# Two self-attentions of a decoder: the second half of each round of heads placed one quarter later

## What is computed

```
q, k, v = split_heads(x @ Wqkv + b)
att = softmax(q @ k.T / sqrt(8))          # per batch entry and head, 256 x 256
y   = att @ v
x   = x + merge_heads(y) @ Wproj + b
```

## The kernel before, in words

| quarter | TensorE | ScalarE | VectorE |
|---|---|---|---|
| 0 | S, T, W of group it-3 | exponential, copy of F | maxima |
| 1 | S, T, every fourth round R | exponential, copy of W | maxima |
| 2 | S, T, M of group it-1, B of group it-3 | exponential | maxima, shift |
| 3 | S, T, F of group it+2 | exponential | maxima, division |

## Time and profile before

### The profile page before, as it was taken

One profiled execution on the slowest core, in us unless ns is written; L12 is line 12 of the kernel. 1 busy time (PEld: TensorE's weight loads), 2 busy tenths in 40 slices (PEclk: granted clock), 3 DMA queues, 4 the chain that ended last, 5 costly groups with the idle time before them and its releaser, 6 DMA issues.

```text
span 939.7 us, 19518 instructions
## 1 busy us (share of the span) xinstructions
PE 847.7 (90%) x6498; PEld 695.7 (74%) x6498; DVE 561.1 (60%) x1561; ACT 480.4 (51%) x1154; POOL 256.1 (27%) x541
## 2 busy tenths in 40 slices
PE   5999879999999999999999968885897888887788
PEld 3888668888888888888888756663796566665565
DVE  3876466555655566655655347774544577666474
ACT  2455465555555555555555315664464476677141
POOL 3864120000000000000000047551075577776110
PEclk9999999999999999999999989999899899999995
DMA  7000000000000000000000030001222000000000
GB/s 270 2 2 1 1 1 1 1 1 1 0 0 0 0 0 0 0 0 0 0 0 0 1 115 1 2 1 28 88 47 59 1 1 0 0 0 0 24 1 22
DMA packets 9410, 15.85 MB, mean 17 GB/s; under 512 B 816, under 2 KB 5040, under 8 KB 8976
## 3 DMA queue, kind: packets, MB, share of 16 engines
q1 hardware_dynamic: 8400, 13.23, 4.2%
q0 software_dynamic: 960, 1.97, 0.9%
HBM read 13.16 MB, written 2.03 MB: 16 GB/s over the span
## 4 chain that ended last, share of the span: by engine, by line
PE 76%; ACT 7%; DVE 6%; issue 6%; POOL 3%; DMA 1%; ACTq 1%; DVEq 0%; POOLq 0%; SPq 0%
PE psum L875 9%; PE psum L887 9%; PE psum L855 5%; PE psum L856 5%; PE psum L857 5%; PE psum L847 5%; PE psum L598 4%; ACT arena L1301 4%; PE psum L840 3%; PE psum L617 3%; PE psum L635 3%; PE psum L956 2%; PE psum L566 1%; PE psum L1034 1%; PE psum L648 1%
## 5 line engine op out<-in xcount | busy, mean ns | idle before, releaser
L1818 DVE TENSOR_REDUCE xnegmax<-psum 128x1 f32<-128x768 f32 x128 | 122.4, 956 | 139.5 <-PE psum L857 139.3
L1405 ACT ACTIVATE arena<-psum,xnegmax 128x768 f32<-128x768 f32 x128 | 115.5, 903 | 139.5 <-DVE xnegmax L1818 97.8
L2265 POOL COPY acur<-A_all 128x128 f32 (+1 forms) x18 | 5.2, 293 | 388.1 <-PE psum L840 388.1
L875 PE MATMUL psum<-pack_a,arena 128*128 128x128 f32 x768 | 106.8, 275 | 0.2 <-ACT arena L1396 0.2
L1249 ACT ACTIVATE arena<-psum 128x384 f32<-128x384 f32 (+1 forms) x128 | 69.5, 546 | 71.2 <-PE psum L620 42.1
L855 PE MATMUL psum<-kv_high,xq_high 128*128 128x384 f32 x256 | 101.5, 396 | 1.8 <-DVE kv_low L1813 1.6
L875 PEld LDWEIGHTS psum<-pack_a,arena 128*128 128x128 f32 x768 | 87.5, 141 | 13.9 <-issue 12.3
L1396 ACT ACTIVATE arena<-psum 128x512 f32<-128x512 f32 x128 | 75.9, 593 | 42.5 <-PE psum L875 42.5
L887 PE MATMUL psum<-arena,xv 128*64 128x256 f32 x768 | 89.9, 383 | 0.0
L856 PE MATMUL psum<-kv_low,xq_high 128*128 128x384 f32 x256 | 86.8, 339 | 0.0
L857 PE MATMUL psum<-kv_high,xq_low 128*128 128x384 f32 x256 | 86.7, 339 | 0.0
(11 more groups left out here) (309 smaller groups left out, 1853.6 us busy)
## 6 DMA issues: line engine op xcount, KB each, us to landing
w1all<-in_w SPq DMA_DIRECT2D x1, 2048.0 KB, 8.2
arena<-in_w SPq DMA_DIRECT2D x1, 2048.0 KB, 10.8
pack_v<-in_pack_v SPq DMA_DIRECT2D x1, 1088.0 KB, 9.0
pack_l<-in_pack_l SPq DMA_DIRECT2D x1, 1079.5 KB, 12.0
pack_q<-in_pack_q SPq DMA_DIRECT2D x1, 1024.0 KB, 6.9
pack_a<-in_pack_a SPq DMA_DIRECT2D x1, 653.0 KB, 6.1
pack_f<-in_pack_f SPq DMA_DIRECT2D x1, 556.0 KB, 9.9
x<-in_x SPq DMA_DIRECT2D x2, 256.0 KB, 3.0
```

What stands on the lines that cost most here:

```text
L875: last = transpose(bank[4 + (3 * u + c) % 2][:, (2 * i + h) * P:(2 * i + h + 1) * P], xprob[:, u % 2, h * KEYS + kt * P:h * KEYS + (kt + 1 ...
L1405: activation(xprob[:, u % 2, half * KEYS:(half + 1) * KEYS].rearrange("p (c w) -> p c w", c=2), src, ACT.Exp, bias=xnegmax[:, u % 2, half: ...
L1818: v.tensor_reduce(xnegmax[:, u % 2, half:half + 1], banks_pair(half), AX.XY, ALU.max, negate=True)\
```

## The change

TensorE's `LAG` goes from 8 to 9 heads. W moves from quarter 0 to quarter 1, R from 1 to 2, M and B from 2 to 3. On ScalarE the exponentials follow `LAG`, and the copies of W and R move from quarter 1 to 2. On VectorE the shift moves from quarter 2 to 3, right behind M's new place, and the division from quarter 3 of a round to quarter 1 of the next. VectorE's loop gets one more round for it. S, F, the copy of F and all of GpSimd's work stay in place, and no DMA moves.

```diff
-LAG = 8
+LAG = 9
...
-                        if j == 0 and 0 <= it - 3 < H:
+                        if j == 1 and 0 <= it - 3 < H:
                             weighted(it - 3)
-                        if j == 1 and it >= 7 and (it - 7) % G == 0:
+                        if j == 2 and it >= 7 and (it - 7) % G == 0:
                             result_turned((it - 7) // G)
...
-                        if j == 2 and 0 <= it - 1 < H:
+                        if j == 3 and 0 <= it - 1 < H:
                             maxima_turned(it - 1)
-                        if j == 2 and 0 <= it - 3 < H:
+                        if j == 3 and 0 <= it - 3 < H:
...
                             back_to_tokens(it - 3)
...
-                        if j == 1 and 0 <= it - 3 < H:
+                        if j == 2 and 0 <= it - 3 < H:
                             empty_weighted(it - 3)
-                        if j == 1 and it >= 7 and (it - 7) % G == 0:
+                        if j == 2 and it >= 7 and (it - 7) % G == 0:
                             result_ready((it - 7) // G)
...
-                for it in range(H + 3):
+                for it in range(H + 4):
...
-                        if j == 2 and 0 <= it - 1 < H:
+                        if j == 3 and 0 <= it - 1 < H:
                             shifted_queries(it - 1)
-                        if j == 3 and 0 <= it - 3 < H:
-                            divided(it - 3)
+                        if j == 1 and 0 <= it - 4 < H:
+                            divided(it - 4)
```

## The result

The changed kernel takes **947.06 us**, the median of 10 runs (945.04 to 954.7), against 941.12 for ten runs of the kernel before beside it. Of both kernels some runs last about 8 us longer than the rest (of the ten, three after the change and one before), and without those the medians are 946.04 and 941.05, +5.0 us; two runs of the kernel before beside later experiments, of 1631 and 1669 us, are left out throughout.

The account below looks back on a forecast made before the run. The prediction took TensorE's queue to bound the kernel, with waits for ScalarE in attention 1. It added 3.5 us for W's wait and 0.3 for the ends to 941.05, giving 944.9 us, range 942.7 to 947.0.

Parts of the forecast that it names:

- W's wait, twelve rounds, 3.5 us: Attention 1, rounds 3 to 14: with F moved, W waits for ScalarE's exponential, +0.29 us a round, 3.5 us.
- M's wait stays: Attention 1: M still starts 1.39 us after the first T behind W, behind ScalarE's copy; gain none.
- Faster: Rival, 0.06: in attention 1 the quarter's delay, not the copy, releases M's hole; -5.0 us, 936.1 us.
- Hidden: Rival, 0.10: W waits at no cost in attention 1, queue or exponential being quicker; only the ends remain, 941.3 us.
- The ends of attention 1, +0.12: Attention 1's first and last rounds: early S costs no time, missing S gives 0.24 back, P before T adds 0.36.
- Attention 0, +0.21: Attention 0's end: P in round 16 now precedes T, +0.21 us; its main rounds cost 0.
- slower still: Rival, 0.06: attention 0's 0.22 us to spare is eaten, W waits about 0.2 us in 12 rounds, 947.3 us.
- the division's move: VectorE: the division gets two quarters instead of one, with the next B a whole round away; no cost.
- 3.5 + 0.3 = +3.8 us: Whole kernel: attention 1's twelve rounds plus the ends of both attentions, added to the median 941.05, give 944.9 us.
- cut a little: Range: 943.3 to 946.5, widened by half the three runs' 1.84 us spread either side, trimmed to 942.7 to 947.0.

Follow-up runs that it names:

- The repeat: The changed kernel timed once more, unaltered, against the kernel before: 946.84 us, ratio 1.0031, beside 941.7 us.

## Why the prediction was right in its steps and short in its size

The direction, the cause and nearly every term held, and 947.06 still lies just outside the range that ended at 947.0.

- *W's wait, twelve rounds, 3.5 us.* Measured: +0.29 for the first (9.61 to 9.90) and +3.13 for the eleven others, 3.42. T to W is 1.09 us, as taken from the earlier trace rows, and F's own place is the cause.
- *M's wait stays.* Right: 1.40 us behind T, 11 holes, 5.5 us. Right also that the copy behind the exponential sets it, which removing that order proved. "Faster" falls: M's hole wasn't the split's. The Trainium skill, "Perfetto Trace Analysis", in Matmuls, asks for independent groups to rotate through different PSUM banks, so that the emptying of one overlaps the products of the next. The trace agrees: M and W share bank 5, and M stands idle for 5.5 us behind W's copy. Here turning two instructions around on ScalarE was enough; another bank wasn't tried.
- *"Hidden".* Refuted: the drained end's row was the geometry of every round.
- *The ends of attention 1, +0.12.* Measured +0.28. W of round 15 to 16 went from 4.62 to 4.38 us (the missing S, -0.24, as forecast); the next went from 4.42 to 4.94, +0.52 instead of +0.36: P starts 0.22 us behind B, where T started 0.13 behind it, and T to W is 1.17 us instead of 1.09 (B, P, T and W start at 645.25, 645.47, 646.28 and 647.45).
- *Attention 0, +0.21.* Measured +0.35, the end +0.22 of it. The rounds were costed at 0 and grew by 0.13; W doesn't wait there, so "slower still" didn't come about by W. What the prediction costed at nothing was the division's move ("covered by the same distance"), and it named B as the one that would wait. It was R of round 7. VectorE's timeline after, with the statistics of the context that now precede the division:

```profile
56.59 0.38 DVE L1545 BATCH_NORM_AGGREGATE stat<-moments 128x2 f32<-128x6 f32 x4
...
57.92 0.20 DVE L1629 RECIPROCAL arena<-psum 128x8 f32<-128x8 f32 x1
58.16 0.23 DVE L1633 TENSOR_TENSOR arena<-psum,arena 128x64 f32<-128x64 f32 x1
```

and the wait of TensorE's weight load for R, from 57 to 59 us:

```profile
PEld psum L666 <- DVE arena L1633: 0.3, 1, 0.3
```

The two loops together: 0.35 + 0.29 + 3.13 + 0.28 = 4.05 us against 3.8 in the sum. The mean span of three traces of the kernel before is 939.3 us, that of four of the changed one 944.8: +5.5, of which the loops are 4.1 and the operand stretch 1.3 (mean 7.67 before, 8.97 after); 0.1 is left.

**The step that failed** is the sum's last: "3.5 + 0.3 = +3.8 us", set straight on the median, takes everything behind the loops as unchanged. The stretch behind attention 0 can run at either clock level and took 1.58 us more or so at the lower (8.72 against 7.14); no term and no bound stood for it, and in the traces it makes 1.3 of the 5.5 us. Whether the change brings that or the executions fell so stays open. The second miss is in the range: half the spread of three runs (1.84 us) was taken as what a measurement adds, and even that was "cut a little", from 947.4 to 947.0; the ten of the changed kernel spread over 9.7 us, and with that their median can move by 1 us. The repeat's 946.84 would have lain inside the range, so on which side of its end the median fell is luck. That 5.0 to 5.9 us were measured where 3.8 were forecast is the miss.

## What to carry to other kernels

In an in-order queue, independent work between a producer and the instruction that waits for another engine's answer is cover: before moving a step, count what stands between the two and compare that with the latency, here 1.09 us from T to W, of which an S and a T cover 0.88 and F the rest. When a wait shows, look first at what the answering engine does in between: putting one copy ahead of one exponential shortened the span from 939.7 to 926.8 us, by three times what the change lost in the two loops. And a busy share says little: TensorE counted as busy for 60.04 of 60.34 us in attention 0's rounds, yet the copy's place took 2.4 us out of them.

## What the chip showed that was not expected

**One level or the other for the same work.** After attention 0, TensorE is about half busy for 4 us, at a granted clock of 1.00, in both kernels. Windows of the kernel before and of the changed one:

```profile
112.00:116.00 4.00, 2.14 (x25) 1.02 (x23) 2.71 (x13) 1.05 (x3) 1.27 (x2) 1.00 0.02 4
117.30:119.33 2.03, 2.03 (x34) 1.86 (x33) 1.81 (x9) 0.79 (x2) 0.00 (x0) 1.00 0.01 4
```

```profile
112.00:116.00 4.00, 2.10 (x25) 0.99 (x23) 0.86 (x4) 1.09 (x3) 0.00 (x0) 1.00 0.02 4
117.36:120.88 3.52, 3.52 (x33) 3.35 (x32) 2.94 (x13) 1.08 (x2) 1.17 (x2) 0.55 0.01 2
```

The same 2.1 us of work ahead, and the products behind run at 1.00 (2.4 GHz) in one and mostly at the lower level (1.2 GHz) in the other. The Trainium skill, "TensorE: Matmul & The Clock Gate", Part 1, calls the number of slow products at a kernel's start run-variable, puts their cost at under 1% of a typical kernel's span, and advises against fitting to a count. Here the stretch lies inside the kernel; the size agrees (1.5 of 940 us is 0.16%), but in this pair of traces it was a quarter of the change's effect (1.58 of 5.7 us of span).

**Two stretches near the end.** TensorE's level also varies in the last stage, from layer 1's self-attention to the end. In the profiled execution of the changed kernel with the copy first it took 216.8 us, against 208.5 in the kernel before; the changed kernel with F ahead of W and the copy first shows 216.8 too. Windows over the self-attention part, of the kernel before and of the changed one with the copy first:

```profile
731.25:886.49 155.24, 128.36 (x1056) 98.78 (x1056) 102.16 (x450) 93.42 (x309) 98.53 (x228) 0.98 0.01 4
722.57:881.62 159.05, 132.29 (x1057) 102.57 (x1057) 102.14 (x450) 93.40 (x309) 98.54 (x228) 0.96 0.01 4
```

and over the last 28 to 33 us, in the same order:

```profile
911.29:939.70 28.41, 23.51 (x91) 15.08 (x89) 12.17 (x44) 3.21 (x6) 1.26 (x2) 0.66 0.06 18
906.50:939.40 32.90, 27.97 (x91) 18.01 (x89) 12.16 (x44) 3.21 (x6) 1.26 (x2) 0.55 0.05 16
```

The same products take 3.8 us more in the first stretch, at a mean granted clock of 0.96 instead of 0.98, and 4.5 more in the second, at 0.55 instead of 0.66. Between the two the time is the same (24.9 and 24.8 us). What decides it wasn't tried.
